# A routed last expert layer: token rows scattered through DRAM to 39 tiles in place of a dense pass

## What is computed

```
def _L3_ffn_ref(hidden_states, gate_w, W1, W2, W3, dom):      # H=128, I=512, E=8
    router_logits = x @ gate_w                                # x: 2048 x 128
    top_logits, top_idx = jax.lax.top_k(router_logits, 2)
    weights = jax.nn.softmax(top_logits, axis=-1)
    w_dense = jnp.einsum('tk,tke->te', weights, jax.nn.one_hot(top_idx, E))
    for e in range(E):
        xe = x + dom[e]
        h = jax.nn.silu(xe @ W1[e]) * (xe @ W3[e])
        out = out + w_dense[:, e:e + 1] * (h @ W2[e])
```

## Time and profile before

| | |
|---|---|
| median of 3 runs | 4088.11 us (4081.66 to 4088.88) |
| profiled execution, span from first to last instruction | 4096.1 us |
| mean granted TensorE clock | 0.907 |
| PE busy | 3535.7 us, 86% |
| DVE busy | 2806.2 us, 69% |
| ACT busy | 1995.0 us, 49% |
| POOL busy | 1465.8 us, 36% |
| last stage (normalisation to the end) | 430.7 us |

### The profile page before, as it was taken

The page is one execution under the profiler, slowest core; times in us unless marked ns, Lnnn a source line. Parts: engine busy times, 40 slices in busy tenths (PEclk is TensorE's granted clock), DMA queues, the critical chain, the costliest instruction groups (busy, mean ns, idle before and its releaser), DMA issues. The chain is left out here.

```text
span 4096.1 us, 127849 instructions
## 1 busy us (share of the span) xinstructions
PE 3535.7 (86%) x55448; PEld 2690.1 (66%) x55640; DVE 2806.2 (69%) x5003; ACT 1995.0 (49%) x3765; POOL 1465.8 (36%) x1373
## 2 busy tenths in 40 slices
PE   6676859999999999999999967989998677669998
PEld 2224448888888888888888845767777552236555
DVE  7994568787777787787787746555555258984454
ACT  5452236666666666666666633444444315531222
POOL 2661035455445444454444422222233104650000
PEclk9897879999999999999999976788888678988999
DMA  0000011011011011011111100000000000010000
GB/s 15 0 1 18 1 64 41 26 46 40 26 45 39 26 45 39 27 46 36 28 28 28 28 7 5 6 7 7 8 7 5 8 7 0 1 62 1 0 0 10
DMA packets 55720, 85.23 MB, mean 21 GB/s; under 512 B 13050, under 2 KB 32532, under 8 KB 54036
## 3 DMA queue, kind: packets, MB, share of 16 engines
q1 hardware_dynamic: 55188, 77.36, 6.3%
HBM read 30.87 MB, written 1.05 MB: 8 GB/s over the span
## 5 line engine op out<-in xcount | busy, mean ns | idle before, releaser
L1924 POOL TENSOR_TENSOR local_rot<-local_term 128x512 f32<-128x512 f32 x384 | 480.5, 1273 | 858.8 <-DVE local_term L2275 858.8
L2275 DVE TENSOR_TENSOR local_term<-bank,local_table 128x512 f32<-128x512 f32 x768 | 486.3, 683 | 114.6 <-ACT local_sq L2155 112.8
L1930 POOL TENSOR_TENSOR local_rot<-local_rot,local_inv 128x512 f32<-128x512 f32 x384 | 399.7, 1062 | 66.8 <-ACT local_inv L2166 45.2
L272 POOL TENSOR_TENSOR mamba_hc<-mamba_state,mamba_c_all 128x512 f32<-128x512 f32 x256 | 326.2, 1296 | 252.7 <-DVE mamba_state L496 237.5
L1953 PE MATMUL bank<-local_w_layer,local_xs 128*128 128x256 f32 x1536 | 367.3, 382 | 4.9 <-ACT local_xs L2149 3.5
L1953 PEld LDWEIGHTS bank<-local_w_layer,local_xs 128*128 128x128 f32 x1536 | 278.8, 192 | 36.3 <-ACT local_xs L2149 3.9
L496 DVE TENSOR_TENSOR_SCAN mamba_state<-bank,mamba_dbu 128x512 f32<-128x512 f32 x256 | 298.0, 1204 | 0.0
L333 PE MATMUL bank<-mamba_hc,ident 128*128 128x512 f32 x512 | 266.4, 646 | 24.0 <-DVEq L505 18.3
L798 DVE SCALAR_TENSOR_TENSOR moe_prod<-bank,moe_b,moe_silu 128x512 f32<-128x512 f32 x160 | 120.1, 751 | 243.5 <-ACT moe_silu L778 242.6
L419 ACT ACTIVATE bank<-mamba_dt,mamba_a_neg 128x510 f32<-128x510 f32 x256 | 176.3, 689 | 225.8 <-DVE mamba_state L496 222.8
L733 PEld LDWEIGHTS bank<-moe_w,moe_gated 128*128 128x128 f32 x1568 | 204.1, 196 | 124.0 <-DVE moe_gated L807 78.7
(11 more groups left out here) (356 smaller groups left out, 8295.4 us busy)
## 6 DMA issues: line engine op xcount, KB each, us to landing
local_v_moved<-local_v_at SPq DMA_DIRECT2D x192, 198.0 KB
local_w_layer<-a_w_layer_dram SPq DMA_DIRECT2D x6, 1536.0 KB, 7.2
local_v_moved<-local_v_at SPq DMA_DIRECT2D x192, 33.0 KB
moe_w<-f_w_dram SPq DMA_DIRECT2D x3, 2048.0 KB, 17.6
local_w_o<-a_w_o_dram SPq DMA_DIRECT2D x6, 512.0 KB, 3.8
local_w_up<-a_w_up_dram SPq DMA_DIRECT2D x6, 341.0 KB, 4.0
moe_w<-f_w_dram SPq DMA_DIRECT2D x3, 576.0 KB, 5.2
delta_w_h<-g_w_qkv_dram SPq DMA_DIRECT2D x8, 192.0 KB, 2.3
```

Source lines behind the costliest of these rows:

```text
L272: ins = pool.tensor_tensor(hc[:, n % 2, h, :], state[:, n % 2, h, :], c_all[:, n % 2, :], ALU.mult)
L1924: pool.tensor_tensor(rot[:, s % 2, :, f, :], here[:, :, f, :], there[:, :, 1 - f, :], ALU.add).then_inc(summed, 1)
L1930: pool.tensor_tensor(one, one, spread(inv[:, s % 2, heads], E), ALU.mult).then_inc(normalized, 1)
L2275: dve.tensor_tensor(term[:, which, b, :], g.bank[b][:, :], table[:, which, :, :].rearrange("p n c -> p (n c)"), ALU.mult).then_inc(roped, 1)
```

## The change

The last `moe` is replaced by `routed_mlp`, which also writes the output; `store` goes. In words:

- DVE marks the two chosen experts of each token. PE multiplies the marks by a matrix of ones and by a strictly triangular one: that counts, for each token and expert, how many tokens before it chose the same. DVE turns counts into places: each expert's rows start at a multiple of 128, so 4096 rows fit in 39 tiles of 128. It also finds each tile's expert (`owner`).
- POOL copies each normalised token row twice into `rows`, with the number of its place in the result behind the 128 features, and scatters the rows through 32 indirect DMAs to `rows_dram`. SP waits for all of them, then loads 3 tiles at a time into `x_in` (13 loads).
- For each of the 39 tiles PE turns the rows, multiplies by `w1[e]` and `w3[e]` (512 columns each), turns the gated result back (4 transposes) and does the 4 down products. The expert `e` is read into a register on PE and on ACT, which adds `dom[e]` while it copies the turned rows. POOL scatters each tile's result to `y_dram`; unused rows carry a number out of bounds and are not written.
- SP reads `y_dram` back when all 39 have landed; DVE adds the two results of a token with their weights, and SP stores group by group.
- In `set_up` SP fills `rows_dram` (4992 rows of 132 numbers) with zeros and the out-of-bounds number.

```diff
@@ set_up
             sp.wait_ge(loaded, 16)
+            sp.wait_ge(filled, 6)
+            sp.dma_start(g.rows_dram.rearrange("(n p) r -> p n r", p=P),
+                         g.fresh[:, :].unsqueeze(1).to_broadcast([P, 39, g.row])).then_inc(g.rows_filled, 16)
...
+            pool.memset(g.fresh[:, :], 0.0).then_inc(filled, 1)
+            pool.wait_ge(filled, 5)
+            pool.iota(g.fresh[:, D:D + 1].bitcast(I32), pattern=[[0, 1]], base=g.unpicked, channel_multiplier=0).then_inc(filled, 1)
@@ build
-            moe(nc, g, "moe3", d_in["f3"], 8, 32, lambda j: j // 4, False, False, True)
-        store(nc, g, out_dram)
+            routed_mlp(nc, g, d_in["f3"], out_dram)
@@ routed_mlp
+        def _(sp):
+            sp.wait_ge(scattered, 16 * PICKS * TILES)
+            for i, some in enumerate(LOADS):
+                sp.dma_start(x_in[:, some, :], g.rows_dram[some.start * P:some.stop * P, :].rearrange("(n p) r -> p n r", p=P)
+                             ).then_inc(x_loaded[i], 16)
+            for i in range(4):
+                sp.wait_ge(y_stored[i], 16 * len(range(i, SLOT_TILES, 4)))
...
+        def _(pool):
...
+            pool.wait_ge(placed, 1)
+            for t in range(TILES):
+                for k in range(PICKS):
+                    pool.indirect_dma_start(out=g.rows_dram[:, :], out_offset=bass.IndirectOffsetOnAxis(ap=slot_of[:, k, t:t + 1], axis=0),
+                                            in_=rows[k][:, t, :], in_offset=None, bounds_check=SLOTS - 1, oob_is_err=False
+                                            ).then_inc(scattered, 16)
+            for i in range(SLOT_TILES):
+                pool.wait_ge(x_loaded[i // 3], 16)
+                pool.wait_ge(out_copied, i + 1)
+                pool.indirect_dma_start(out=g.y_dram[:, :],
+                                        out_offset=bass.IndirectOffsetOnAxis(ap=x_in[:, i, D:D + 1].bitcast(I32), axis=0),
+                                        in_=y_out[:, i % 4, :], in_offset=None, bounds_check=PICKS * N - 1, oob_is_err=False
+                                        ).then_inc(y_stored[i % 4], 16)
...
+        def _(pe):
...
+            pe.matmul(g.bank[2][:, 0:E * TILES], every[:, :], all_chosen, start=True, stop=True).then_inc(counted, 1)
+            pe.matmul(g.bank[1][:, 0:E * TILES], before[:, :], all_chosen, start=True, stop=True).then_inc(counted, 1)
...
+            def go_up(i, e):
+                pe.wait_ge(xt_ready, i + 1)
+                pe.wait_ge(s_ready, i) if i else None
+                pe.matmul(g.bank[H_BANK][:, :], xt[:, i % 2, :], w1[:, bass.ds(e, 1), :].rearrange("p a n -> p (a n)"),
+                          start=True, stop=True).then_inc(h_ready, 1)
+                pe.wait_ge(gated_ready, i - 1) if i >= 2 else None
+                pe.matmul(g.bank[U_BANK[i % 2]][:, :], xt[:, i % 2, :], w3[:, bass.ds(e, 1), :].rearrange("p a n -> p (a n)"),
+                          start=True, stop=True).then_inc(u_ready, 1)
...
+            for i in range(SLOT_TILES + 2):
+                if i < SLOT_TILES:
+                    experts[i] = pe.value_load(owner[0:1, i:i + 1], min_val=0, max_val=E - 1)
+                    go_up(i, experts[i])
+                if i + 2 < SLOT_TILES:
+                    turn_rows(i + 2)
+                if 0 <= i - 1 < SLOT_TILES:
+                    turn_gated(i - 1)
+                if i >= 2:
+                    go_down(i - 2, experts.pop(i - 2))
...
+        def _(dve):
...
+            own.step(dve.tensor_tensor_scan(upto[:, :, :].rearrange("p e t -> p (e t)"), keep[:, :, :].rearrange("p e t -> p (e t)"),
+                                            totals, 0.0, ALU.mult, ALU.add))
...
+            dve.tensor_copy(slot_of[:, :, :], slot_f[:, :, :]).then_inc(placed, 1)
...
+            def copy_out(i):
+                dve.wait_ge(out_ready, i + 1)
+                dve.wait_ge(y_stored[i % 4], 16 * (i // 4)) if i >= 4 else None
+                dve.tensor_copy(y_out[:, i % 4, :], g.bank[O_BANK[i % 2]][:, 0:D]).then_inc(out_copied, 1)
```

More of the change, by code:

```diff
@@ L2398, in _ @@
             dve.wait_ge(added, 1)
[L2401 to L2410, removed]
 STAGES = (0, 1, 2, 3, 4, 5, 6, 7)
@@ L2426, in build @@
         g.gate_weights, g.gate_weights_due = ctx.enter_context(nc.semaphore("gate_weights")), 0
+        g.row, g.unpicked = D + 4, 1 << 20
+        g.rows_dram = nc.dram_tensor("rows_dram", [39 * P, g.row], F32, kind="Internal").ap()
+        g.y_dram = nc.dram_tensor("y_dram", [2 * N, D], F32, kind="Internal").ap()
+        g.fresh, g.rows_filled = sb("fresh", [P, g.row]), ctx.enter_context(nc.semaphore("rows_filled"))
         set_up(nc, g, d_in["x"])
@@ L2507, in lay_out @@
             "gate_w": i["L3_ffn_gate_w"], "dom": i["L3_ffn_dom"].T,
-            "w1": i["L3_ffn_W1"].transpose(1, 0, 2).reshape(D, 32, P),
-            "w3": i["L3_ffn_W3"].transpose(1, 0, 2).reshape(D, 32, P),
-            "w2": rows(i["L3_ffn_W2"].reshape(-1, D)),
+            "w1": i["L3_ffn_W1"].transpose(1, 0, 2), "w3": i["L3_ffn_W3"].transpose(1, 0, 2),
+            "w2": rows(i["L3_ffn_W2"].reshape(-1, D)).reshape(P, 8, 4 * D),
         },
```

207 lines of the change are left out of this document (added).

## The result

The changed kernel takes 3881.5 us (median of 4 runs, 3876.4 to 3887.9), the kernel before 4086.9 in the same session (4081.7 to 4088.9). The ratio is 0.950, 95% interval 0.948 to 0.952: 205 us faster. The forecast was 3906 with a range of 3862 to 3985. Sign and mechanism were right, and the gain was 23 us larger than forecast; between the two profiled executions 7.4 of it lie in code that was not changed. The profiled execution after is the slowest of the four, span 3886.1 us; its sum in the prediction was 3913.7.

A forecast was written before the change was run, and what follows sets the result against it. The prediction took dense matmul work on PE as the bound. Its terms made a new last stage of 244.8 us against 430.7 (-185.9), -182.4 with the start: 3913.7 profiled, 3905.7 for the median, range 3862 to 3985.

The forecast's parts named there:

- What stays: Start of the last stage, kept from the old kernel: normalisation, gate matmuls at half clock and ranking, 24.7 us.
- (a) places: Computing each row's place after ranking: DVE comparisons, two counting matmuls on PE, 14 small DVE steps; 6.1 us.
- (b) scatter: 32 indirect DMAs issued one after another by POOL, 41.6 us, plus 2.0 to land, all on the path.
- c: Price of one indirect DMA on POOL, taken as 1.3 us; ends for the range 0.8 and 3.
- The rival of a dearer c: POOL's DMAs do not overlap, c = 2.3, and only the first scatter shows it: 32 us more, 3938; chance 0.15.
- (d) 39 tiles of 3.6: Expert loop: 3.16 us of PE work per tile plus 0.44 for the register load, 140.4 us for 39 tiles.
- two of the 0.24 'issue' gaps: In each tile, PE's register load priced at 0.44 us, one gap for the read and one for its use.
- (c) first load and filling: Between scatter and loop: first load of rows 2.3 us, filling the pipeline 6.0, together 8.3.
- (e): The tail: last tile drains 3.0, last scatter 1.3 plus 2.0, read-back 9.2, adds 2.4, store 3.3, clearing 0.5; sum 21.7 us.
- (f) the start: Kernel start: SP's 2.6 MB fill delays the first mamba stage's weights on the same queue, 3.5 us; ends 0 and 10.
- Clock (0.08): Rival: TensorE's clock falls to half in the tile loop, 123 us more, 4029; half of it 3967; chance 0.08.
- POOL (0.05): Rival: POOL bounds scatter and loop, above 3.6 us per DMA in the loop; slower than before from 5.1; chance 0.05.

The follow-up runs named there:

- experiment 2: Changed kernel with 16 scatters instead of 32 (each token's second choice not sent); last stage 203.9 us against 223.9.
- experiment 3: Changed kernel with 32 scatters of 64 rows instead of 128; last stage 221.4 us against 223.9, a scatter 909 ns mean against 976.
- experiment 1: Changed kernel with each tile's expert fixed at build, without register loads on PE and ACT; last stage 224.4 us against 223.9.
- experiment 7: Changed kernel working 33 tiles instead of 39, rows placed behind them left out; last stage 205.0 us against 223.9.
- Experiment 10: Changed kernel with weights carried in the scattered rows and 8 plain additions instead of 32 scaled ones; last stage 222.0 us, median 3892.0.
- experiment 4: Changed kernel with each tile's result scattered three times, 117 indirect DMAs in the loop instead of 39; last stage 256.3 us against 223.9.
- experiment 8: Changed kernel with the fill of rows_dram moved behind the first stage; second stage starts at 325.1 us instead of 327.7, last stage 225.1.
- experiment 11: Changed kernel with carried weights, later fill, nine unused products on waiting TensorE and a one-tile first load; last stage 222.6 us, median 3888.3.

## Why the prediction was right, and where it was off

- **The bound** (dense matmul work that shortens one for one) held, and the three stretches came as forecast.
- **What stays, and (a) places:** 30.8 forecast, 30.0 measured.
- **(b) scatter:** 43.6 forecast, 42.0 measured. c is 1.27, not 1.3, and experiment 2 puts it on the path. Its reason, 128 addresses computed one by one, fell in experiment 3. That the size came out so near was luck: it was taken from POOL's rows of another kind. The rival of a dearer c (0.15) fell in the timeline: the next DMA starts 1.27 us behind one that lands after 2.3, so they overlap. The Trainium skill's 2.0 us fixed and 436 bytes per ns ("DMA: Bandwidth & Descriptors", section "Anatomy of one DMA — SWDGE (gpsimd) path") give an estimated 2.16 for 67.6 KB, close to the measured 2.3 to landing. It is a latency and not the spacing of the queue, so the 27 us that adding it up would have cost did not come.
- **(d) 39 tiles of 3.6** is the step that failed. The term "two of the 0.24 'issue' gaps" a tile was 17.2 us for nothing: the lower bound, "0, if queued matmuls hide it", is what happens, shown by experiment 1 and by experiment 7's 3.16 a tile. 3.16 itself was right to the hundredth. (Two of 0.24 are also 0.48 and not 0.44, which would have added 1.6 us.)
- **(c) first load and filling, with the drain of (e):** from the landing of the last scatter to the last result's copy it was 8.3 + 140.4 + 3.0 = 151.7, and measured 130.1. Less the 17.2 above, 4.4 are left: filling and draining took 6.9 us beyond the 39 tiles' 123.2, where I had 11.3. The first load took 2.8 instead of 2.3, and the drain's 3.0 fits (126.2 from the first up product to the last copy's end, less 123.2). The filling's 6.0, taken from the old loop, was the error: 1.1 us behind the first turned row the first up product starts, and although the clock stays at 0.50 until 3743 and the table load follows, the last tile's L961 starts at 3858.40, only 0.2 behind 3738.11 + 38 x 3.16: PE doesn't have transposes and downs of earlier tiles beside its first two. That reading of the timeline was not tested by a run of its own.
- **(e) the rest of the tail:** 18.7 forecast, 21.8 measured. The first group's rows are there 3.7 us after the read-back's first issue, but SP needs 5.2 us for eight issues, and the 32 additions, 9.1 us in all (2.31 + 6.76), run behind the loads and hold back the stores. I had counted only the last group's, 2.4. Experiment 10 shows what fewer and larger additions give back: 2.0.
- **(f) the start:** 3.5 forecast, 4.0 in this pair, about 2.9 over all executions, so not far off. The place was not as named: it is the queue's next issue that stands still.
- **Clock (0.08) and POOL (0.05) rivals:** the clock was 0.97 in the loop. (The slices with PE at 7 tenths, named against the first rival, show clocks of 6 to 9 tenths, not 7 to 9.) POOL becomes the bound at three DMAs a tile (experiment 4), as the other rival has it, though from 3.16 us a tile on and not from 3.6.
- **Sum:** stage 223.9 against 244.8 (-20.9), start +0.5, untouched stages -7.4, in all -27.8, against 27.6 between 3913.7 and the measured span; the rest is rounding. The last part is spread and not knowledge.

## What to carry to other kernels

Before pricing a new small instruction on a bound engine, ask whether it can be done while the matmuls issued in front of it still run. Here the register load cost nothing (experiment 1), and the honest price is zero with the other end in the range. An indirect DMA cost POOL 1.27 us a piece, nearly whatever its rows (experiment 3), so count instructions and not bytes, and check that count against the time it has to hide in. A small edit to a pipeline's start should be read on all engines first: what looks idle may be covering something else.

## What the runs showed of the hardware that I had not expected

- An indirect DMA costs POOL 1.27 us with 128 rows (0.97 + 0.30) and 1.21 with 64 (0.91 + 0.30): nearly all of it is fixed.
- A plain DMA issued on SP's queue right behind a 2.6 MB one takes 6.7 to 7.05 us to issue instead of 0.33 to 0.37 (the kernel after and experiment 8), and holds whatever SP would issue next.
- TensorE's granted clock was 0.50 up to 3744 in experiment 11, 0.81 in the next 4 us and 1.00 from 3748 on, with PE busy from 3740.2. It was 0.63 behind 3755, after 3.7 us with little work (from 3750.8 to 3754.5 two transposes of 0.33).
- The local and delta stages, the same code, took 2707.1 to 2738.5 us. In the delta stage alone it was 806.7 at a granted clock of 0.82 and 831.4 at 0.78. What sets the clock, and the rest of the spread, stays open.
